# GpSimd takes the whole mean subtraction of the convolution's second pass

## The reference

```python
x = L0_attn_x                                   # (8, 4096, 512) float32
xn = (x - mean(x, -1)) / sqrt(var(x, -1) + 1e-5)
q = 1 - sigmoid(delta) * sigmoid(alpha)         # (512, 16, 1)
k = einsum('dnl,dn->dl', sigmoid(delta) * beta * exp(t * log(q)), gamma * sqrt(1/16))
x = x + irfft(rfft(xn^T, 2l) * rfft(k, 2l))[:l]^T + xn * omega
...                                             # then a mixture of 8 experts on the first 4096 tokens
```

## Time and profile before

| | |
|---|---|
| median of 3 runs | 1120.56 us (1119.09 to 1127.54) |
| span of the profiled execution | 1123.9 us |
| pass 0 / expert layer / pass 1 | to about 380 / to about 833 / to 1124 us |
| busy in the whole span: PE, DVE, ACT, POOL | 926.9, 817.0, 785.4, 609.9 us |
| POOL's subtraction, both passes | 128 times, 1117 ns mean |
| DVE's subtraction, both passes | 128 times, 704 ns mean |

### The profile page before, as it was taken

How to read it: one execution, slowest core, us unless ns; L and a number is a source line. 1 busy time by engine, 2 the same in 40 slices (tenths; PEclk the granted TensorE clock), 3 DMA queues, 4 the chain that set the end, 5 groups by cost and what they waited for, 6 DMA issues and landing times. The chain is left out here.

```text
span 1123.9 us, 32990 instructions
## 1 busy us (share of the span) xinstructions
PE 926.9 (82%) x11452; PEld 748.8 (67%) x11452; DVE 817.0 (73%) x1360; ACT 785.4 (70%) x1151; POOL 609.9 (54%) x706
## 2 busy tenths in 40 slices
PE   2770788888779788999999999999987888886881
PEld 1550676767667666777777777777766777675771
DVE  7878897989689333667576676766657989896891
ACT  3772898989779544565656656565577989896890
POOL 5625885868584224566666666666655333332330
PEclk9995898999989888999999999999998999999896
DMA  8998999999999896999999999899749999999986
GB/s 302 396 401 305 256 247 241 271 230 299 305 291 321 230 237 156 258 283 260 291 272 229 241 236 256 221 242 248 180 111 251 217 234 273 232 291 285 316 189 149
DMA packets 392137, 288.01 MB, mean 256 GB/s; under 512 B 125928, under 2 KB 339592, under 8 KB 391554
## 3 DMA queue, kind: packets, MB, share of 16 engines
q1 hardware_dynamic: 346018, 211.68, 69.5%
q0 software_dynamic: 19520, 36.26, 14.8%
q10 hardware_dynamic: 26528, 39.14, 10.7%
HBM read 197.41 MB, written 100.61 MB: 265 GB/s over the span
## 5 line engine op out<-in xcount | busy, mean ns | idle before, releaser
L1476 PE MATMUL ps<-xn,wb 128*128 128x128 f32 x2048 | 275.8, 291 | 0.0
L1078 ACT ACTIVATE cen<-ps 128x1024 f32<-128x1024 f32 x156 | 155.7, 1023 | 168.4 <-PE ps L1571 166.3
L1476 PEld LDWEIGHTS ps<-xn,wb 128*128 128x128 f32 x2048 | 251.0, 200 | 17.5 <-issue 3.3
L582 POOL TENSOR_TENSOR cen<-xb,mean 128x512 f32<-128x512 f32 x128 | 142.9, 1117 | 219.8 <-DVE state L1280 152.5
L1253 DVE TENSOR_TENSOR xn<-cen,rstd 128x1024 f32<-128x1024 f32 x128 | 175.0, 1367 | 50.1 <-POOL cen L582 42.4
L1463 PE MATMUL ps<-xn,near 128*32 128x128 f32 x2048 | 86.6, 289 | 120.9 <-DVE xn L1253 72.6
L1571 PE MATMUL ps<-carry,wb 64*128 64x256 f32 x1248 | 168.7, 400 | 12.8 <-DVE carry L1326 9.0
L1586 PEld LDWEIGHTS ps<-cen,xn 128*64 128x64 f32 x2496 | 136.4, 137 | 38.2 <-ACT cen L1078 31.4
L1586 PE MATMUL ps<-cen,xn 128*64 128x128 f32 x2496 | 160.8, 276 | 0.4 <-ACT cen L1078 0.3
L1264 DVE TENSOR_TENSOR xb<-xb,ps 128x1024 f32 (+1 forms) x128 | 152.8, 1194 | 9.8 <-PE ps L1488 9.8
L977 ACT ACTIVATE wb<-wide 32x1024 f32<-32x1024 f32 x126 | 144.6, 1147 | 15.8 <-DMA wide<-taps_d 13.1
(11 more groups left out here) (173 smaller groups left out, 1273.9 us busy)
## 6 DMA issues: line engine op xcount, KB each, us to landing
xb<-L_attn_x SPq DMA_DIRECT2D x160, 512.0 KB, 9.8
out<-xb SPq DMA_DIRECT2D x72, 512.0 KB, 6.6
xb<-L_attn_x ACTq DMA_DIRECT2D x128, 256.0 KB, 4.9
out<-xb SPq DMA_DIRECT2D x88, 256.0 KB, 4.5
wb<-L_ffn_w_B SPq DMA_DIRECT2D x78, 256.0 KB, 4.3
wide<-taps_d SPq DMA_DIRECT2D x63, 256.0 KB, 5.8
dk<-decay_d SPq DMA_DIRECT2D x63, 128.0 KB, 4.8
out<-y_d SPq DMA_DIRECT2D x4, 1536.0 KB, 12.8
```

Of the source, the lines that this page charges most:

```text
L582: pool.tensor_tensor(cen[:, k, 0:QB // 2].rearrange("p b r d -> p r b d"), unit_view(pool, g, i, k)[:, :, 0:UC // 2] .rearrange("p r (b d) ...
L1078: act.activation(act_h[:, b % 2].rearrange("p f t -> p (f t)"), ps[:, 2 * (b % 2):2 * (b % 2) + 2, :].rearrange("p a t -> p (a t)"), ACT.G ...
L1476: ins = pe.matmul(ps[:, QB * k + b, d * P:(d + 1) * P], wb[:, h, k * QB + b, d, :], xn[:, k, 2 * b + d, :], start=(b > 0 and d == 0), stop ...
```

## The change

In the second pass POOL subtracts the mean for all eight channels of a unit, in one instruction of 1024 elements in place of 512. DVE's `centre` does nothing there, and DVE's `stage` no longer waits for it. The first pass stays as it is. The wait on `s_x` that `centre` had is left to POOL.

```diff
@@ centres, on gpsimd
-                        pool.tensor_tensor(cen[:, k, 0:QB // 2].rearrange("p b r d -> p r b d"),
-                                           unit_view(pool, g, i, k)[:, :, 0:UC // 2]
+                        nb = QB // 2 if g == 0 else QB
+                        pool.tensor_tensor(cen[:, k, 0:nb].rearrange("p b r d -> p r b d"),
+                                           unit_view(pool, g, i, k)[:, :, 0:2 * nb]
                                            .rearrange("p r (b d) -> p r b d", d=2),
                                            mean[:, g * P:(g + 1) * P][:, :, None, None]
-                                           .to_broadcast([P, P, QB // 2, 2]),
+                                           .to_broadcast([P, P, nb, 2]),
                                            ALU.subtract).then_inc(s_cen, 1)
@@ centre, on vector
+                if g == 1:
+                    return
                 u = 2 * i + k
-                if not (g == 0 and isinstance(i, int) and i < BT):
+                if not (isinstance(i, int) and i < BT):
                     wait(dve, s_x, tiles_in(i, g))
@@ stage, on vector
                 wait(dve, s_loc, u - 1)
-                wait(dve, s_cend, u + 1)
+                if g == 0:
+                    wait(dve, s_cend, u + 1)
                 wait(dve, s_cen, u + 1)
```

## The result

The changed kernel takes 1129.9 us, median of 6 runs (1127.97 to 1131.76), beside 1122.23 for the kernel before on the same chips; the ratio is **1.0051, interval 1.0027 to 1.0076**. A second set of runs gave 1.0068 (1.0046 to 1.0091). So it is slower, by 6 to 8 us (3 to 10 by the intervals): inside the range, but only about half of the 12 us that were forecast. Of the 1129.9 us, 1.7 belong to the kernel before, whose median was 1120.56 when the forecast was made; the loss itself is the better measure. The profiled execution took 1127.97 us, its span is 1126.2.

The account below looks back on a forecast made before the run. The second pass was taken as bound by the DVE–POOL loop of xn, scan and POOL's subtraction. Tile losses 4.0 + 3.0 + 0 + 5.2 = 12.2 us on 1120.56 gave 1133 us, range 1121 to 1145.

Parts of the forecast that it names:

- Pace: Second pass's steady loop: POOL's subtraction lies on the path, 2.01 us in place of 1.10; each turn costs 0.30 us more.
- 1.3 us among the signs at its end: Sign expected in the profile after: each xn row of the second pass waits some 1.3 us for POOL.
- Tile 0: Second pass, tile 0: fifth and sixth xn some 2 and 3 us late, seventh +1.25, nine turns 2.7; sum +4.0 us.
- Tile 1: Second pass, tile 1: 13 turns cost 3.9 us, third xn can come 0.9 sooner; sum +3.0 us.
- Tile 2: Second pass, tile 2: its loss of 3.0 us is covered by DVE's 6.68 us wait for tile 3's loads; 0.
- The chain of transfers: SP's tile 2 stores through tile 3's loads landing: 69 us, moves with the start of tile 2 and does not grow.
- rival (D): Transfers catch up, tile 3's loads up to 5 us earlier: 7.2 us, 1128; chance 0.15, shared with an instruction of 1.7 to 1.85.
- Tile 3: Second pass, tile 3: POOL's first subtractions in the open, +1.3 us by the third xn; with 13 turns +5.2 us.
- The account of the two engines taking turns: Start of tile 3: xn meets POOL's second subtraction for 1.9 us, so it takes 2.8 us, ending 1.2 later.
- (A): Rival: POOL's instruction in the second pass simply doubles to 2.19 us, turn +0.48, sum 19.4 us, 1140 us; chance 0.25.
- (B): Rival: POOL's instruction much shorter than its elements say, break-even 1.70 us; at 1.55, 1115 us, not slower; chance 0.05.
- (C): Rival: PE's clock falls with more idle, making PE the bound; 8 to 15 us more, about 1145 us; chance 0.05.

Follow-up runs that it names:

- six and two: Kernel before, but in the second pass POOL subtracts six channels and DVE two: ratio 1.0063 (1.0041 to 1.0084), length of second pass 275.2 us.
- the first pair of profiles: First profiles of the kernel before and the changed kernel: second pass 269.0 us long before, 274.8 after.
- the second profile: Kernel before and changed kernel each profiled again: second pass 269.4 us long before, 275.1 after; changed kernel's ratio 1.0068.
- tile 2 alone: Kernel before, but POOL takes all eight channels only in tile 2 of the second pass: ratio 1.0003 (0.9983 to 1.0023), length 269.4 us.
- tile 3 alone: Kernel before, but POOL takes all eight channels only in tile 3 of the second pass: ratio 1.0033 (1.0011 to 1.0054), length 270.3 us.
- both splits: Second pass without POOL's wait for the scan, on the changed kernel and on the kernel before's 4 and 4 split: 1.0135 and 1.0124 of before.

## Why the prediction was right, and where its sizes were off

**Pace.** Right: POOL's subtraction lies in the turn of xn, scan, subtraction, xn, and its increase shows in every turn. Too large: the turn grew by 0.22 us on average (51.04 for 48.16 in 13 turns of tile 1) and not by 0.30. The row of DVE's xn gives the parts: scan start to POOL start 0.59 as before, POOL 1.96 and not 2.01, and POOL's start to xn only 1.98 to 1.99 us, where 2.01 + 0.10 was taken. The handover is 0.03 us in place of 0.10. The split of six and two, where `stage` keeps its second wait, has 0.10 again (1005.18 + 1.55 to 1006.83), so it went with that wait in the rows read here. The turn beside the copy came out at 4.10 for 4.14 only, since the earlier handover lets xn meet more of the copy: from xn to scan it is 1.53 us there and not 1.44. By the first pair of profiles the turns are 2.5 us of the 6.4 that the forecast was too high. DVE's wait of 1.05 us fits the 1.1 us of the working; the 1.3 us among the signs at its end did not follow from it. POOL's length was chosen from its fixed part of 0.18 with the slope of the same form, and that was nearest; plain doubling gives 2.19. The estimate of 2.2 us from GPSIMD Engine Reference (section 3.1) in the Trainium skill was too dear for this form as well.

**Tile 0.** Here a step failed. +4.0 us were forecast, and the last xn came 1.1 later in the first pair of profiles, 2.3 in the mean of all with that tile (before: 63.8, 63.0, 63.1, 61.3; changed: 64.9, 65.2). The nine turns behind the seventh xn cost 2.4 (35.48 us for 33.10) and not 2.7, so what stands ahead of them is -1.3 in the first pair, about 0 in the mean, and not +1.25. I let every delay of POOL run on through the scatters. But before the third scatter POOL waited for an earlier one to land, as this row of the kernel before shows:

```profile
850.65 0.18 POOL L542 COPY pick_s<-slot_s 128x2 int32<-128x2 int32 x1 [3.62 <-DMA out<-lag,pick_s]
```

After the change that wait is 0.31 us:

```profile
845.34 0.99 POOL L542 COPY pick_s<-slot_s 128x2 int32<-128x2 int32 x1 [0.31 <-DMA out<-lag,pick_s]
```

So the longer subtractions ahead of it were covered, a cover that I had in the trace (3.62 us, and 4.00 in the second profile) and put down as moving along. The fifth xn came at 20.7 and 20.9 us, for 20.9 and 21.3 before, and not 2 late; the sixth at 25.7 and 26.0, for 25.1 and 25.5, and not 3 late. What makes a scatter land earlier or later stays open.

The seventh xn had a second cover. Before, it waited 2.31 us for PE, 1.19 in the second profile. After the change it comes 3.71 us behind the sixth in both profiles, an ordinary turn that waits for POOL alone:

```profile
859.53 1.61 DVE L1257 TENSOR_TENSOR xn<-cen,rstd 128x1024 f32<-128x1024 f32 x1 [1.05 <-POOL cen L583]
```

PE's granted clock does not account for this. In the second profiles it was the same in both kernels, 1.00 from 10 to 25 us behind POOL's first subtraction, 0.66 from 25 to 30 and 1.00 from there on, and the seventh xn waited 1.19 us for PE before the change and not at all after it. PE was busy there for 0.36 us from 20 to 25 us before the change and for 2.04 after it, so its work came earlier; why stays open.

**Tile 1.** +3.0 forecast, +1.9 in the first pair, +1.4 in the mean of the same profiles. The tile change gained 1.0 us (0.9 forecast) in the first pair, 14.58 to 13.60 from the last xn to the third of the next tile and 15.22 to 13.47 in the second; the turns cost 2.9 in place of 3.9.

**Tile 2.** Right: its own loss is covered, as the run with tile 2 alone shows; in the changed kernel its last add ended 3.5 us before tile 3's x landed (6.7 before, near 3.7 forecast). The chain of transfers, forecast as fixed, was 1.3 us shorter than before (68.1 for 69.5 us; 68.1 and 69.7 in the second profiles). That is the way rival (D) would have it, but not shown to be its doing: with tile 3 alone changed, where no turn ahead of the chain is longer, it was 68.4, and with six and two, where all are, 70.0.

**Tile 3.** +5.2 forecast; measured 1.6 to the third xn (1.3 forecast) and 2.7 in the turns (3.9), +4.3 in all, and +4.1 to the end of the last add. The run with tile 3 alone gives 4.2. The account of the two engines taking turns held: the first xn was to take 2.8 us and took 2.88, counted by itself.

**The rivals.** (A), 2.19 us, and (B), a break-even below 1.70, did not occur. (C) did not: the granted clock is 1.00 in the steady part. The size of the loss, 6 to 8 us, is that of rival (D), 7.2, but the transfers gave only 1.3 of the up to 5 us that (D) asks for. In sum the path was the right one, and 12.2 had sizes too large in three places, by the first pair: turns 2.5 us, tile 0's start 2.6 (+1.25 forecast, -1.3 measured), transfers 1.3.

## What to carry to other kernels

When work is moved to an engine that starts only after a step of the receiving engine, time its whole length on the path and not its share of busy time: DVE was freed of 0.60 us a unit, and POOL's extra 0.86 stood in the same turn; with 0.07 saved at the handover a turn grew by 0.19 us, and by 0.24 beside the copy. Before a wait that looks idle is removed, ask what would run beside the released instruction; here the wait kept GpSimd off VectorE's two-input instructions, and without it both splits were 1.2 to 1.4% slower than the kernel before. The gain lay the other way, with the small part on GpSimd (two channels of eight): its 0.67 us in place of 1.10 no longer holds VectorE up, whose own work then sets the turn. That is 0.5% with both passes changed.

## What the runs showed of the hardware

- A GpSimd subtraction and a VectorE instruction with two SBUF inputs exclude each other but for some 0.13 us: a scan of 0.42 us took 2.16 beside a GpSimd subtraction of 1.96. The add with a PSUM input kept 1.18 to 1.22 us in every profile.
- GpSimd's fp32 subtraction with a repeated operand follows 0.24 us + 1.68 ns per element from 256 to 1024 elements, while two sizes of its plain sums (454 ns for 128, 726 for 256) give 0.18 us + 2.13 ns.
- A GpSimd copy of 0.61 us lengthened the xn beside it by the time that they met less some 0.14 us: 0.38, 0.33 and 0.10 us for 0.53, 0.47 and 0.23 us.
- With one semaphore to wait for, VectorE's xn started 0.03 us after the end of GpSimd's subtraction; with two it started 0.10 after it.
